# Token rows of six steps in flight, weight requests in another order, and 26 unread turns on TensorE, in a two-block gated decoder kernel

## The chip, the cores and the metric

The kernel runs on one core of a Trainium2 chip. The metric is the device time of one execution in microseconds (us). Five engines work side by side, each through its own list of instructions: PE (TensorE, matrix products; PEld is its loading of weights), DVE (VectorE), ACT (ScalarE), POOL (GpSimd) and SP (SyncE, which here only issues DMAs). They wait for each other through semaphores. "Granted clock" is the share of 2.4 GHz that TensorE is given; it has two levels, 1.00 and 0.50.

## The reference

Four sequences of 256 tokens with 256 channels pass through four gated parts, each added to x. The changed lines belong to the first two.

```python
# 1: state-space scan over 16 states on the context, gated by silu of the normalised x
x = x + tanh(g_xattn[0]) * scan_block(ctx, layernorm(x), ...)
# 2: mixture of experts: E=64 experts, K=8 per token, at most CAP=64 tokens per expert
logits = layernorm(x) @ gate_w.T
w, sel = top_k(softmax(logits), 8);  w = w / sum(w)
pos  = position of each (token, choice) in its expert's queue     # cumulative sum of one-hots
inp  = rows of x placed at (expert, pos) where pos < 64
h    = silu(inp @ wg[e]) * (inp @ wu[e])                           # 256 -> 96
out  = h @ wd[e]                                                   # 96 -> 256
y[token] += out[expert, pos] * w
# 3: attention of 16 heads over the context
# 4: two ternary linear layers with gelu and layer norm
```

## The kernel before

Everything is in one program with a hand-written instruction list for each engine. The parts that matter here:

*The scan* (up to about 162 us) works on two halves of 512 columns; 64 steps of DVE's scan instruction bound it. TensorE sums the products with turns of the identity (`add_pair`).

*The choice of experts, second half of tokens* (about 162 to 200 us). Behind the scan TensorE turns the gated output (`turn_out(1, b)`), waits while DVE adds it to x and takes the statistics, turns the normalised rows (`turn_normal(1, k)`), waits while ACT copies them out of PSUM, and makes the logits (`logits_of(1)`). Among these stand turns and products for the attention part, which fold its weight matrices (`turn_kv`, `fold_out`, `turn_wq`). DVE picks the experts, TensorE counts positions (`cumulate`, `count`, `lay_out`), and the result is `idx_x`, for each slot of each expert the index of its token row.

*The sixteen expert steps* (about 200 to 280 us). A step is a group of four experts, 256 slots. For step g:
- POOL's `take_rows(g)` gathers 2 x 128 rows of 320 numbers (256 of the token, 64 shares of the experts) from the table `token_rows` in HBM. They go to `xe`, a ring of RING = 4 places in the tile G. From step 4 on it waits for `hg_ready`, the gated product of step g - 4, which has used its rows.
- TensorE turns the rows (`turn_rows`), ACT copies them, TensorE multiplies with both weights (`gate_up`), ACT takes the silu, DVE the product, TensorE turns it (`turn_h`), multiplies with the down weights (`down`, two steps later), and adds the outputs into the token rows of the first sequence (`combine`, three steps later).
- SP's `put` writes the output of a step to the table `expert_out` in HBM, through three result tiles in turn.

In TensorE's list, turn g of the loop holds `turn_rows(g + 1)`, `gate_up(g)`, `turn_h(g - 1)`, `down(g - 2)` and `combine(g - 3)`.

*Weights.* Each group has 2 x 384 KB of gate and up weights and 384 KB of down weights. Groups 0 to 3 fill the ring at the start; 5 to 7 go to `wgu_early` and `wdn_early`, 15 to `wgu_last` and `wdn_last`, all before the stage or at its start. Group 4's gate and up weights go to `wgu_more`, the rest of the tile G behind `xe`, once the attention weights below it have been turned (`wqT_in_psum`). Groups 8 to 14 are requested in SP's loop over s, where each waits for `gu_done` or `down_done` of the group whose place it takes. A DMA issued by SP stands in one queue behind those issued before it.

Of the kernel before, what the change touches and what calls it, by code (L numbers as in the profile page):

```python
# [15 lines left out]
P = 128  # L16
# [24 lines left out]
B, L, H, DM = 4, 256, 256, 128  # L41
# [10 lines left out]
GROUP = 4  # L52
RING = 4
NG = E // GROUP
EARLY = 3
# [5 lines left out]
def build_program(nc, t, out):  # L61

    with ExitStack() as ctx:
# [168 lines left out]
        def gate_up_weights(slot):  # L232

            return (wgu[:, slot] if slot < RING else
                    (wgu_last[:], wgu_more, *(w[:] for w in early_gate_up))[slot - RING])

        def gate_up_slot(g):

            if g == NG - 1:
                return RING  # L240
            if RING <= g <= RING + EARLY:
                return g + 1
            return g % RING

        def down_weights(slot):
            return wdn[:, slot] if slot < RING else (wdn_last[:], None, *(w[:] for w in early_down))[slot - RING]

        def down_slot(g):

            if g == NG - 1:  # L250
                return RING
            if RING < g <= RING + EARLY:
                return g + 1
            return g if g < RING else 0 if g == RING else (g - RING - EARLY) % RING
# [5 lines left out]
        xe_flat = G[:].rearrange("p a k h -> p (a k h)")[:, 0:RING * 2 * ROW]  # L260
        wgu_more = G[:].rearrange("p a k h -> p (a k h)")[:, RING * 2 * ROW:].rearrange("p (a e i) -> p a e i", a=2, e=GROUP)
# [57 lines left out]
        def gate_up_landed(g):  # L319

            if g < RING:
                return d_w[g], 48
            if g == NG - 1:
                return d_ffn, 48
            if g == RING:
                return d_zero, 64
            if g <= RING + EARLY:
                return early_landed[g - RING - 1]
            return d_w[g % RING], 48 + 32 * (g // RING - 1)

        def down_landed(g):

            if g < RING:
                return d_w[g], 48
            if g == NG - 1:
                return d_ffn, 48
            if RING < g <= RING + EARLY:
                return early_landed[g - RING - 1]
            s, before = down_ring[down_slot(g)]
            return s, before + 16 * (1 if g < 12 and g != 11 else 2)  # L340
# [35 lines left out]
        d_gath = [[sem(f"d_gath{cc}{half}") for half in range(2)] for cc in range(2)]  # L376
        eo_hi_ready, eo_lo_ready = sem("eo_hi_ready"), sem("eo_lo_ready")
# [48 lines left out]
        def _(sp_):  # L426
# [21 lines left out]
            def gate_up_load(g):  # L448

                slot = gate_up_slot(g)  # L450
                if g == RING:
# [3 lines left out]
                landed = gate_up_landed(g)[0]  # L455
                for k, name in enumerate(("L0_ffn_wg", "L0_ffn_wu")):
                    dma(gate_up_weights(slot)[:, k],
                        t[name][g * GROUP:g * GROUP + GROUP].rearrange("e (p j) i -> p e (j i)", j=2))\
                        .then_inc(landed, 16)

            def down_load(g):

                if g == RING:
                    sp_.wait_ge(down_done, 1)
                elif RING + EARLY < g < NG - 1:
                    sp_.wait_ge(down_done, g - 6 if g < 12 else g - 3)
                dma(down_weights(down_slot(g))[0:I], t["L0_ffn_wd"][g * GROUP:g * GROUP + GROUP]
# [16 lines left out]
            gate_up_load(NG - 1)  # L484
            down_load(NG - 1)
# [32 lines left out]
            gate_up_load(RING)  # L518
# [2264 lines left out]
```

## Time and profile before

| | |
|---|---|
| median of 3 runs | 581.57 us (579.41 to 582.18) |
| the profiled execution | 579.86 us |
| its span, first to last instruction | 577.9 us |
| mean granted clock | 0.953 |
| busy: PE, DVE, ACT, POOL | 83%, 82%, 63%, 49% of the span |
| DMA | 48.63 MB, 84 GB/s over the span |
| the chain that ended last | PE 37%, DVE 21%, issue 20%, POOL 9%, ACT 7%, DMA 3% |

The profile is of one execution. The chain goes back from the last instruction to what released it, or to the one before it on its engine. "Issue" is time in which an engine waited for nothing that the profile shows. In a timeline a row's bracket is the engine's idle time before it and what ended it. PE records begin when a product begins; their ends overlap the next. A window has, for each engine, busy time and the number of instructions, then the granted clock, the DMA engines' share and the rate in GB/s. One `matmul` with 32-bit numbers over several columns can be two records.

### The profile page before, as it was taken

How to read it: one execution, taken by the hardware profiler on the slowest of the kernel's cores; microseconds unless marked ns; L12 is line 12 of the kernel's file. 1: busy time of each engine (PE TensorE's matmuls, PEld its weight loads, DVE VectorE, ACT ScalarE, POOL GpSimd, SP SyncE). 2: the span in 40 equal slices, each digit the busy share in tenths (PEclk: the TensorE clock that was granted, in tenths of full speed). 3: DMA queues.
4: the chain of work that ended last, by engine and by line, in shares of the span. 5: the costliest groups of instructions: out<-in, count | busy, mean ns of one | idle time of the engine just before them, and what ended most of it. 6: DMA issues, size and time to landing. Idle time of an engine off the chain costs nothing.

```text
span 577.9 us, 10286 instructions
## 1 busy us (share of the span) xinstructions
PE 478.6 (83%) x3070; PEld 361.1 (62%) x3080; DVE 473.6 (82%) x1249; ACT 365.2 (63%) x831; POOL 280.9 (49%) x263
## 2 busy tenths in 40 slices
PE   5817777757769889999899999998789988998735
PEld 3302222122348856776788999997689878997714
DVE  4899999999995737888666856996899969875887
ACT  2785555535434645688776666679656796679543
POOL 4118777869420465550278368623875243323211
PEclk9956999999997989999999999999999999999877
DMA  5939400001052979894412012400335000000000
GB/s 155 233 76 325 120 0 1 1 1 36 1 157 80 308 217 294 212 313 144 180 52 73 2 29 65 56 1 2 47 55 66 0 2 2 19 2 0 1 19 20
DMA packets 45626, 48.63 MB, mean 84 GB/s; under 512 B 5660, under 2 KB 42118, under 8 KB 45574
## 3 DMA queue, kind: packets, MB, share of 16 engines
q1 hardware_dynamic: 41734, 36.46, 22.2%
q0 software_dynamic: 3840, 11.54, 9.3%
q8 instruction: 25, 0.41, 0.3%
q14 instruction: 27, 0.22, 0.1%
HBM read 41.43 MB, written 6.56 MB: 83 GB/s over the span
## 4 chain that ended last, share of the span: by engine, by line
PE 37%; DVE 21%; issue 20%; POOL 9%; ACT 7%; DMA 3%; SPq 1%; DVEq 1%; POOLq 0%; ACTq 0%; another core or an unknown queue 0%
DVE hst L1880 7%; PE ps L1619 6%; PE ps L1558 5%; PE ps L1559 5%; PE ps L1560 5%; PE ps L1608 3%; PE ps L1476 2%; DMA G<-token_rows,idx_x 2%; POOL dbu L586 2%; PE ps L1277 2%; POOL G L672 2%; POOL pn L688 2%; DVE hc L1889 2%; POOL G L650 1%; PE ps L1374 1%
## 5 line engine op out<-in xcount | busy, mean ns | idle before, releaser
L688 POOL TENSOR_TENSOR pn<-pr,pinv 128x512 f32<-128x512 f32 x64 | 67.7, 1060 | 87.3 <-DVE pinv L2289 86.9
L586 POOL TENSOR_TENSOR dbu<-du,brow 128x512 f32<-128x512 f32 x64 | 81.5, 1285 | 41.4 <-DVE du L1873 23.1
L1277 PE MATMUL ps<-hc,ident 128*128 128x512 f32 x128 | 72.7, 657 | 27.5 <-DVE hc L1889 26.0
L1880 DVE TENSOR_TENSOR_SCAN hst<-ps,dbu 128x512 f32<-128x512 f32 x64 | 77.6, 1213 | 0.2 <-POOL dbu L586 0.2
L831 ACT ACTIVATE ps<-dtv,amat 128x510 f32<-128x510 f32 x64 | 44.1, 690 | 49.1 <-DVE hst L1880 48.2
L1019 ACT ACTIVATE pr<-ebuf,smin 128x256 f32<-128x256 f32 x128 | 63.7, 501 | 13.7 <-DVE smin L2280 6.9
L1619 PE MATMUL ps<-pT,cS 128*128 128x256 f32 x256 | 66.5, 382 | 0.0
L1277 PEld LDWEIGHTS ps<-hc,ident 128*128 128x128 f32 x128 | 20.3, 195 | 66.8 <-DVE hc L1889 63.6
L650 POOL DMA_INDIRECT G<-token_rows,idx_x x32 | 38.1, 1192 | 48.3 <-DVE wkv L2015 24.0
L672 POOL DMA_INDIRECT G<-expert_out,idx_g x48 | 51.6, 1074 | 11.6 <-issue 10.2
L2280 DVE CUSTOM_DVE_ANT_0 ebuf<-ps,mbias 128x256 f32<-128x256 f32 x128 | 48.9, 419 | 4.1 <-issue 4.0
L1558 PE MATMUL ps<-xnT,mqk 128*128 128x256 f32 x128 | 46.3, 362 | 6.7 <-DVE qT L2250 3.5
L1608 PE MATMUL ps<-ident,pn 128*128 128x128 f32 x256 | 39.4, 277 | 9.1 <-POOL pn L688 5.2
L1619 PEld LDWEIGHTS ps<-pT,cS 128*128 128x128 f32 x256 | 44.3, 191 | 3.7
L1033 ACT ACTIVATE oT<-ps 128x256 fp32r<-128x256 f32 x64 | 24.4, 382 | 31.8 <-PE ps L1619 31.7
L1558 PE MATMUL ps<-cT,qT 128*128 128x256 f32 x128 | 41.5, 324 | 1.4 <-DVE smin L2280 1.2
L1889 DVE TENSOR_TENSOR hc<-hst,ps 128x512 f32<-128x512 f32 x64 | 42.1, 659 | 0.0
L1027 ACT ACTIVATE pT<-ps 128x512 f32<-128x512 f32 x64 | 37.3, 583 | 4.3 <-PE ps L1608 4.2
L1558 PE MATMUL ps<-nvo,oT 128*128 128x256 f32 x128 | 37.2, 291 | 2.5 <-DVE oT L2250 2.5
L2250 DVE TENSOR_TENSOR oT<-ps,oT 128x256 fp32r<-128x256 f32 x64 | 26.7, 418 | 15.1 <-ACT oT L1033 14.8
L1608 PEld LDWEIGHTS ps<-ident,pn 128*128 128x128 f32 x256 | 29.1, 142 | 12.6 <-POOL pn L688 6.5
L1012 ACT ACTIVATE qT<-ps 128x256 fp32r<-128x256 f32 x64 | 24.6, 384 | 19.1 <-PE ps L1560 19.1
(380 smaller groups left out, 1377.3 us busy)
## 6 DMA issues: line engine op xcount, KB each, us to landing
wdn<-in_L_ffn_wd SPq DMA_DIRECT2D x12, 384.0 KB, 9.6
wgu<-in_L_ffn_wg SPq DMA_DIRECT2D x11, 384.0 KB, 7.0
wgu<-in_L_ffn_wu SPq DMA_DIRECT2D x11, 384.0 KB, 9.7
expert_out<-xn SPq DMA_DIRECT2D x11, 256.0 KB, 6.8
wq<-in_L_xattn_Wq SPq DMA_DIRECT2D x2, 1024.0 KB, 9.2
wo<-in_L_xattn_Wo SPq DMA_DIRECT2D x1, 2048.0 KB, 15.7
wo<-in_L_ffn_w SPq DMA_DIRECT2D x2, 1024.0 KB, 7.0
expert_out<-pexp SPq DMA_DIRECT2D x5, 256.0 KB, 3.3
```

The lines of the kernel that those rows point to most:

```text
L586: nc.gpsimd.tensor_tensor(dbu[:, j, :], du[:, j % 2, 512 * hb:512 * hb + 512], brow[:, j // 2, :], ALU.mult).then_inc(pool_dbu, 1)
L672: nc.gpsimd.indirect_dma_start(G[:, cc, k, :], None, eout, bass.IndirectOffsetOnAxis(ap=idx_g[:, col:col + 1], axis=0), bounds_check=SLOTS ...
L688: nc.gpsimd.tensor_tensor(pn[:, h % 2], pr[:, h % 2], pinv[:, h % 2, :].unsqueeze(2).to_broadcast([P, 2, L]), ALU.mult)\
L831: A(bank(d).rearrange("p (b l) -> p b l", b=2)[:, :, 1:], dtv[:, d, 512 * hb:512 * hb + 512].rearrange("p (b l) -> p b l", b=2)[:, :, 1:], ...
L1019: last = A(pr[:, h % 2, tt, :], sneg[:, h % 2, tt, :], ACT.Exp, scale=-1.0, bias=smin[:, h % 2, tt:tt + 1], accum_out=psum_[:, h % 2, tt:t ...
L1277: pe.matmul(bank(2 + j % 2), ident[:], hc[:, j % 2, :], start=(isinstance(m, int) and m + k == 0), stop=(isinstance(m, int) and m + k == N ...
L1558: pe.matmul(o, lhs[0], rhs[0], start=start, stop=False)
L1608: last = pe.transpose(ps[:, 4, L * st + P * tt:L * st + P * tt + P], pn[:, h % 2, tt, P * st:P * st + P], ident[:])
L1619: last = pe.matmul(ps[:, 3 + 2 * (h % 2), 0:L], cS[:, b % 2, st, :], pT[:, h % 2, st, :], start=(st == 0), stop=(st == 1))
L1880: V.tensor_tensor_scan(hst[:, j, :], bank(j % 2), dbu[:, j, :], 0.0, ALU.mult, ALU.add)\
L1889: V.tensor_tensor(hc[:, j % 2, :], hst[:, j, :], bank(6 + j // 2), ALU.mult).then_inc(hc_ready, 1)
L2280: last = V.tensor_tensor_reduce(sneg[:, h % 2, tt, :], ps[:, 1, L * tt:L * tt + L], mbias[:, b, :], -(DH ** -0.5), 3e38, ALU.add, ALU.min, ...
```

## The change

Four things:
1. `xe` gets ROWS = 6 places instead of four. `take_rows(g)` waits for the gate of step g - 6; steps 4 and 5 wait for `wqT_in_psum`, since their places were group 4's weights. The two new places use the semaphores of the later gathers, `d_gath[0]`, whose counts in `add_choices` start 64 higher.
2. Homes of weights: group 4 takes what was group 15's (`wgu_last`, `wdn_last`), and groups 8 to 15 follow in a ring of five. `wgu_more` is gone.
3. SP requests group g's gate and up weights in turn (6g - 36) // 5 + 1 of its loop, the down weights one turn later.
4. On TensorE, `gate_up(1)` and `gate_up(2)` stand ahead of `turn_rows(2)` and `turn_rows(3)`; and `keep_busy` turns the identity into a PSUM tile that nobody reads, 12, 9 and 5 times, at three places of the choice of experts. It was there before, with 24 such turns written out, behind the expert steps.

```diff
+ROWS = 6
-        xe = G[:].rearrange("p a k h -> p (a k h)")[:, 0:RING * 2 * ROW].rearrange("p (s q w) -> p s q w", s=RING, q=2)
-        wgu_more = G[:].rearrange("p a k h -> p (a k h)")[:, RING * 2 * ROW:].rearrange("p (a e i) -> p a e i", a=2, e=GROUP)
+        xe_flat = G[:].rearrange("p a k h -> p (a k h)")[:, 0:ROWS * 2 * ROW]
+        xe = xe_flat.rearrange("p (s q w) -> p s q w", s=ROWS, q=2)
+        def home(g):
+            if g < 2 * RING:
+                return g
+            return (g - 2 * RING) % (RING + 1)
...
             def gate_up_load(g):
-                if g == RING:
-                    sp_.wait_ge(wqT_in_psum, NKV)
-                elif RING + EARLY < g < NG - 1:
-                    sp_.wait_ge(gu_done, g - 7 if g < 12 else g - 3)
+                if g > RING + EARLY:
+                    sp_.wait_ge(gu_done, g - 7 if g <= 3 * RING else g - 4)
...
-            gate_up_load(NG - 1)
-            down_load(NG - 1)
+            gate_up_load(RING)
+            down_load(RING)
...
             down_load(RING + 1)
-            gate_up_load(RING)
             for s in range(NG + 2):
-                if s < 2:
-                    gate_up_load(s + 8)
-                if s == 2:
-                    down_load(RING)
-                    gate_up_load(10)
...
+                for g in range(2 * RING, NG):
+                    if s == (6 * g - 36) // 5 + 1:
+                        gate_up_load(g)
+                    if s == (6 * g - 36) // 5 + 2:
+                        down_load(g)
                 if s > 1:
                     put(s - 2)
...
             def take_rows(g):
-                if g >= RING:
-                    pool.wait_ge(hg_ready, g - RING + 1)
+                if g >= ROWS:
+                    pool.wait_ge(hg_ready, g - ROWS + 1)
+                elif g >= RING:
+                    pool.wait_ge(wqT_in_psum, NKV)
...
+            def keep_busy(k, count):
+                for _ in range(count):
+                    pe.transpose(ps[:, k, 0:P], ident[:], ident[:])
...
             turn_kv(1)
+            pe.wait_ge(b_copied, 2 * NS)
+            keep_busy(4, 12)
             turn_out(1, 0)
...
             fold_out(1)
+            keep_busy(6, 9)
             turn_normal(1, 0)
             turn_normal(1, 1)
+            keep_busy(4, 5)
             logits_of(1)
...
             for g in range(NG + 3):
+                if g in (1, 2):
+                    gate_up(g)
                 if g + 1 < NG:
                     turn_rows(g + 1)
-                if 0 < g < NG:
+                if 2 < g < NG:
                     gate_up(g)
```

TensorE behind the scan, before: `ps<-ident,wkv` is `turn_kv`, `ps<-ident,u` is `turn_out`, `ps<-wo,w2T` is `fold_out`, `ps<-ident,xn` is `turn_normal`, `ps<-gwT,dtv` is `logits_of`.

```order
L1366 MATMUL ps<-ident,wkv 128x128 x8
L1289 MATMUL ps<-ident,u 128x128 x8
...
L1374 MATMUL ps<-wo,w2T 128x256 x4
L1301 MATMUL ps<-ident,xn 128x128 x8
L1310 MATMUL ps<-gwT,dtv 128x64 x8
L1374 MATMUL ps<-wo,w2T 128x256 x4
```

The same place in the changed kernel, where `ps<-ident` is a filler:

```order
L1346 MATMUL ps<-ident,wkv 128x128 x8
L1258 MATMUL ps<-ident 128x128 x12
L1269 MATMUL ps<-ident,u 128x128 x8
...
L1354 MATMUL ps<-wo,w2T 128x256 x4
L1258 MATMUL ps<-ident 128x128 x9
L1281 MATMUL ps<-ident,xn 128x128 x8
L1258 MATMUL ps<-ident 128x128 x5
L1290 MATMUL ps<-gwT,dtv 128x64 x8
L1354 MATMUL ps<-wo,w2T 128x256 x4
```

Nothing else has moved there; 26 rows were added.

TensorE at the start of the expert steps, before (`ps<-ident,G` turns rows, `ps<-wgu,ebuf` is gate and up, `ps<-ident,ebuf` is `turn_h`, `ps<-wdn,hT` is down):

```order
L1464 MATMUL ps<-ident,G 128x128 x4
L1476 MATMUL ps<-wgu,ebuf 64x192 x8
L1464 MATMUL ps<-ident,G 128x128 x4
L1541 MATMUL ps<-wabs,ones 128x2
L1464 MATMUL ps<-ident,G 128x128 x4
L1476 MATMUL ps<-wgu,ebuf 64x192 x8
L1487 MATMUL ps<-ident,ebuf 96x128 x2
L1464 MATMUL ps<-ident,G 128x128 x4
L1476 MATMUL ps<-wgu,ebuf 64x192 x8
L1487 MATMUL ps<-ident,ebuf 96x128 x2
L1497 MATMUL ps<-wdn,hT 64x256 x4
```

And in the changed kernel:

```order
L1448 MATMUL ps<-ident,G 128x128 x4
L1459 MATMUL ps<-wgu,ebuf 64x192 x8
L1448 MATMUL ps<-ident,G 128x128 x4
L1525 MATMUL ps<-wabs,ones 128x2
L1459 MATMUL ps<-wgu,ebuf 64x192 x8
L1448 MATMUL ps<-ident,G 128x128 x4
L1470 MATMUL ps<-ident,ebuf 96x128 x2
L1459 MATMUL ps<-wgu,ebuf 64x192 x8
L1448 MATMUL ps<-ident,G 128x128 x4
L1470 MATMUL ps<-ident,ebuf 96x128 x2
L1479 MATMUL ps<-wdn,hT 64x256 x4
```

Gate and up of steps 1 and 2 now stand ahead of the turning of the rows of the step after.

SP's list behind the request of group 5, before (`expert_out<-` rows are puts):

```order
L457 DMA G<-in_L_ffn_wg 128x4x192
L457 DMA G<-in_L_ffn_wu 128x4x192
L457 DMA wgu<-in_L_ffn_wg 128x4x192
L457 DMA wgu<-in_L_ffn_wu 128x4x192
L457 DMA wgu<-in_L_ffn_wg 128x4x192
L457 DMA wgu<-in_L_ffn_wu 128x4x192
L467 DMA wdn<-in_L_ffn_wd 96x4x256
L457 DMA wgu<-in_L_ffn_wg 128x4x192
L457 DMA wgu<-in_L_ffn_wu 128x4x192
L511 DMA expert_out<-xn 128x2x256
```

And in the changed kernel:

```order
L493 DMA expert_out<-xn 128x2x256
L441 DMA wgu<-in_L_ffn_wg 128x4x192
L441 DMA wgu<-in_L_ffn_wu 128x4x192
L493 DMA expert_out<-xn 128x2x256
L449 DMA wdn<-in_L_ffn_wd 96x4x256
L441 DMA wgu<-in_L_ffn_wg 128x4x192
L441 DMA wgu<-in_L_ffn_wu 128x4x192
L493 DMA expert_out<-pexp 128x2x256
```

Nine requests (3.5 MB) that stood ahead of the first put are behind it or, those of group 4, far ahead of the stage.

## Rows read from the trace of the kernel before

**Rows 1.** Timeline of TensorE, 146 to 206 us: start us, us, engine, line, operation [idle before].

```profile
151.97 1.89 PE L1310 MATMUL ps<-gwT,dtv 128*128 128x64 f32 x16
...
164.86 1.09 PE L1289 MATMUL ps<-ident,u 128*128 128x128 f32 x8 [1.86 <-DVE u L2045]
...
167.53 1.97 PE L1374 MATMUL ps<-wo,w2T 128*128 128x256 f32 x8
170.86 1.38 PE L1301 MATMUL ps<-ident,xn 128*128 128x128 f32 x8 [1.36 <-DVE xn L2054]
172.93 3.67 PE L1310 MATMUL ps<-gwT,dtv 128*128 128x64 f32 x16 [0.69 <-ACT dtv L850]
176.39 3.50 PE L1374 MATMUL ps<-wo,w2T 128*128 128x256 f32 x8
...
183.06 0.19 PE L1330 MATMUL ps<-ebuf,through 128*128 128x64 bf16 x1
```

**Rows 2.** Windows: PE, PEld, DVE, ACT, POOL busy, granted clock, DMA share, GB/s.

```profile
164.00:166.00 2.00, 1.14 (x10) 1.15 (x11) 1.93 (x6) 0.00 (x0) 0.26 (x1) 1.00 0.04 6
172.00:174.00 2.00, 1.31 (x7) 1.08 (x7) 1.93 (x12) 1.32 (x3) 0.00 (x0) 0.68 1.13 288
206.00:208.00 2.00, 1.44 (x8) 1.03 (x10) 0.00 (x0) 0.38 (x1) 1.39 (x3) 0.71 1.12 370
```

**Rows 3.** Timeline of TensorE from 200 us, columns as in rows 1.

```profile
200.42 0.74 PE L1464 MATMUL ps<-ident,G 128*128 128x128 f32 x4 [0.69 <-ACT mqk_full L861]
201.94 1.52 PE L1476 MATMUL ps<-wgu,ebuf 128*64 128x192 f32 x16 [0.78 <-ACT ebuf L919]
203.39 0.75 PE L1464 MATMUL ps<-ident,G 128*128 128x128 f32 x4
...
206.56 1.03 PE L1464 MATMUL ps<-ident,G 128*128 128x128 f32 x4 [2.30 <-DMA G<-token_rows,idx_x]
207.51 2.83 PE L1476 MATMUL ps<-wgu,ebuf 128*64 128x192 f32 x16
...
224.25 0.75 PE L1464 MATMUL ps<-ident,G 128*128 128x128 f32 x4 [1.17 <-DMA G<-token_rows,idx_x]
...
228.81 0.64 PE L1464 MATMUL ps<-ident,G 128*128 128x128 f32 x4
...
232.20 0.39 PE L1512 MATMUL ps<-eo_hi,place 128*128 128x256 f32 x1
...
233.25 0.65 PE L1464 MATMUL ps<-ident,G 128*128 128x128 f32 x4
...
280.35 2.79 PE L1554 MATMUL ps<-ident 128*128 128x128 f32 x24
```

**Rows 4.** Chain of waits, 140 to 290 us: start us, us, what.

```profile
215.79 8.42 DMA G<-token_rows,idx_x
```

**Rows 5.** Timelines of ACT and of DVE, 155 to 212 us, columns as in rows 1.

```profile
178.45 0.60 ACT L861 ACTIVATE nvo_full<-ps 128x512 f32<-128x512 f32 x1 [5.09 <-PE ps L1374]
...
180.93 0.30 DVE L1948 TENSOR_SCALAR ebuf<-left 128x256 bf16<-128x256 f32 x1
```

**Rows 6.** Timeline of POOL, 190 to 262 us, one gather of 128 rows each.

```profile
194.93 1.28 POOL L650 DMA_INDIRECT G<-token_rows,idx_x  x1 [23.96 <-DVE wkv L2015]
...
205.21 1.00 POOL L650 DMA_INDIRECT G<-token_rows,idx_x  x1 [0.30 <-issue]
...
211.88 1.00 POOL L650 DMA_INDIRECT G<-token_rows,idx_x  x1 [3.05 <-DVE ebuf L2136]
```

**Rows 7.** Line L650, the row gathers that began at 206 to 208 us.

```profile
DMA to landing us min/median/max: 3.0/3.6/4.5
```

**Rows 8.** Windows in the expert steps, columns as in rows 2.

```profile
214.00:216.00 2.00, 2.00 (x20) 1.54 (x20) 1.19 (x5) 1.93 (x4) 1.39 (x3) 1.00 0.89 194
...
250.00:260.00 10.00, 10.00 (x87) 7.55 (x86) 9.32 (x18) 8.37 (x19) 4.72 (x4) 1.00 1.10 298
```

**Rows 9.** DMA issues at 223 to 224 us: engine, operation, count, size, us to landing.

```profile
expert_out<-pexp SPq DMA_DIRECT2D x1, 256.0 KB, 10.9
```

More of the change, by code:

```diff
@@ L230, in build_program, with gate_up_weights, down_weights @@
         prep_scope.close()
[L232 to L254, printed above, removed]
+        gate_up_homes = [*(wgu[:, k] for k in range(RING)), wgu_last[:], *(w[:] for w in early_gate_up)]
+        down_homes = [*(wdn[:, k] for k in range(RING)), wdn_last[:], *(w[:] for w in early_down)]
+        def home(g):
+            if g < 2 * RING:
+                return g
+            return (g - 2 * RING) % (RING + 1)
+        def gate_up_weights(g):
+            return gate_up_homes[home(g)]
+        def down_weights(g):
+            return down_homes[home(g)]
         G = sb("G", [P, 2, K, H])
-        xe = G[:].rearrange("p a k h -> p (a k h)")[:, 0:RING * 2 * ROW].rearrange("p (s q w) -> p s q w", s=RING, q=2)
-        xe_flat = G[:].rearrange("p a k h -> p (a k h)")[:, 0:RING * 2 * ROW]
-        wgu_more = G[:].rearrange("p a k h -> p (a k h)")[:, RING * 2 * ROW:].rearrange("p (a e i) -> p a e i", a=2, e=GROUP)
+        xe_flat = G[:].rearrange("p a k h -> p (a k h)")[:, 0:ROWS * 2 * ROW]
+        xe = xe_flat.rearrange("p (s q w) -> p s q w", s=ROWS, q=2)
         spare = sb("spare", [P, 2])
@@ L322, in gate_up_landed @@
                 return d_w[g], 48
-            if g == NG - 1:
+            if g == RING:
                 return d_ffn, 48
-            if g == RING:
-                return d_zero, 64
             if g <= RING + EARLY:
                 return early_landed[g - RING - 1]
-            return d_w[g % RING], 48 + 32 * (g // RING - 1)
+            if home(g) == RING:
+                return d_ffn, 48 + 32 + 32
+            return d_w[home(g)], 48 + 32 * (1 if g < 3 * RING else 2)
         def down_landed(g):
[L333 to L340, printed above, removed]
+            if g <= RING + EARLY:
+                return gate_up_landed(g)
+            if home(g) == RING:
+                return d_zero, 32 + 16
+            s, before = down_ring[home(g)]
+            return s, before + 16 * (1 if g < 3 * RING else 2)
         d_rows = sem("d_rows")
@@ L658, in _ @@
             pool.wait_ge(idx_x_ready, 1)
-            for g in range(RING):
-                take_rows(g)
-            for g in range(RING, NG):
+            for g in range(NG):
                 take_rows(g)
@@ L1498, in down @@
                                          hT[:, g % 2, P * q + CAP * e:P * q + CAP * e + CAP],
-                                         down_weights(slot)[0:I, 2 * q + e, :], start=True, stop=True)
+                                         down_weights(g)[0:I, 2 * q + e, :], start=True, stop=True)
                 last.then_inc(down_done, 1)
@@ L1708, in tail_turn_hidden @@
                 last.then_inc(f_hqT_in_psum, 1)
-            def keep_busy(k, count):
-                for _ in range(count):
-                    pe.transpose(ps[:, k, 0:P], ident[:], ident[:])
             def tail_out(k, first=0, end=FT):
@@ L2210, in add_choices @@
                     if k < 2:
-                        dve.wait_ge(d_gath[cc][half], 8 * K * b)
+                        dve.wait_ge(d_gath[cc][half], 8 * K * b + (0 if cc else 64))
                 if k > 1:
```

38 lines of the change are left out of this document (13 added, 25 removed).

## The prediction

> **What bounds the kernel now.** I read the page's forty slices for stretches in which no engine is full, then the chain of waits from 140 to 290 us, then TensorE's timeline in the two stretches that the change touches, and last the windows for the granted clock and the DMA rate. The two stretches are the choice of experts of the second half of the tokens (162 to 200 us) and the sixteen expert steps (200 to 284 us). Before and behind them nothing is changed, so everything behind them should only move with them.
>
> In the first stretch TensorE is busy without a gap from 172.93 on, but it starts that run slowly. It idles 1.86 us before the turns at 164.86, 1.36 before those at 170.86 and 0.69 before the logits at 172.93 [rows 1]. The granted clock is 1.00 (2.4 GHz) at 164 to 166, and falls to the half level (1.2 GHz) within 172 to 174 (mean 0.68) [rows 2]. The same logits that take 1.89 us at 151.97 take 3.67 at 172.93, and four folding products that take 1.97 at 167.53 take 3.50 at 176.39 [rows 1].
>
> In the second stretch a step of TensorE is 4.45 us (228.81 to 233.25), of which the combining products are the last 1.05 (232.20 to 233.25); a step without them is 3.40. From 224.25 on the steps follow with hardly a gap. Before that they don't: 2.30 us are lost before 206.56 and 1.17 before 224.25, both to token rows that had not landed, and gate-and-up of step 1 takes 2.83 us instead of 1.52 [rows 3], because the first of these waits let the clock fall to a mean of 0.71 in 206 to 208 [rows 2]. The piece of the chain that ends in the second wait is a landing of 8.42 us [rows 4]. That is the landing of step 6's rows. So this stage is TensorE's, apart from a ragged start.
>
> **The fillers.** They add 12, 9 and 5 turns that nobody reads. The 24 turns of the same kind at 280.35 take 2.79 us [rows 3], 0.116 each, so the three fillers are 1.40, 1.05 and 0.58 us and stand in gaps of 1.86, 1.36 and 0.69. Each begins when its gap begins: the wait on b_copied that the first brings forward has long been met (its last copy belongs to the scan, which has ended), and the instruction behind each filler waits for something from DVE or ACT that the filler doesn't touch. What hides them is these waits, with 0.46, 0.31 and 0.11 us to spare. Without that cover they would cost up to 3.03 us, at the half clock twice that. I take 0.
>
> What they may give is the clock. If it doesn't fall, the logits get back 3.67 - 1.89 = 1.78 us and the four products 3.50 - 1.97 = 1.53, together 3.31. Does another engine stand in the way? ACT's copy at 178.45, which waited 5.09 us for TensorE's products, sits ahead of the exponentials; it follows TensorE. DVE's choice at 180.93 begins 2.48 us behind that copy and takes 0.30 [rows 5]. With the faster clock TensorE ends the first pair of products near 172.93 + 1.78 + 0.95 = 175.7; the choice is then ready at 175.7 + 2.48 + 0.30 = 178.5. TensorE wants it for the counting products, which began at 183.06 [rows 1], now 3.31 earlier at 179.75. So 1.25 us are to spare and TensorE stays the bound up to the row indices. The row gathers on POOL begin at 194.93 behind these [rows 6] and come 3.3 us earlier too; so do the stage's weight requests, all of them behind waits on TensorE. Bounds: 0 if the clock falls all the same, 3.31 if it holds, and -1.5 if a filler runs late. I take 3.3, since all three gaps shrink to less than half a microsecond, and TensorE held full clock at 164 to 166, right behind its longest gap [rows 1, 2].
>
> The engine's turns in the gaps are themselves transposes, as are those at 164.86, and the clock read 1.00 around them. The Trainium skill (TensorE: Matmul & The Clock Gate, "Part 4: PE-mode transpose") says against this that the full clock does not engage for the transpose mode. By that rule the fillers give nothing, and the sum would end 3.3 us later; by the rows it holds. It is part of the first rival below.
>
> **Six steps of rows in flight, and two gate-and-ups moved ahead.** From here I count in the time of the old trace, leaving the 3.3 out. Turns to gate-and-up is 201.94 - 200.42 = 1.52 us (ACT copies between them), gate-and-up is 203.39 - 201.94 = 1.45 [rows 3]. In the old order gate-and-up of step 1 stands behind the turns of step 2 and so behind their late rows. In the new one it stands ahead: start 203.39 + 1.52 = 204.91, end 206.36. The rows of step 2 had landed at 206.51 and should land a little earlier, since two requests for weights that stood in front (those of group 4 and of group 8) are gone from there. Turns of step 2 at 206.4, gate-and-up of step 2 at 207.9 to 209.35, then the rest of a step without combining, 3.40 - 1.45 = 1.95, gives 211.3. Step 3 and step 4 at 4.45 (or 3.40 + 1.05) give 215.75 and 220.2 for the start of step 5, the one that began at 224.25. That is 4.05 us. It holds the 2.30 and 1.17 of waiting and the slow clock of 207 to 210 less the 0.7 and 0.6 us of new idling while ACT copies; these are too short to bring the clock down again, to judge by 164 to 166.
>
> Do the rows keep up? POOL issues a gather in 1.00 us and 0.30 between two; the eighth, at 205.21, stands 10.28 us behind the first, so 1.47 each at the worst [rows 6]. A step is 2.6 to 2.9 us, less than a step of TensorE. In the old order step 5's rows waited 3.05 us at 211.88 for step 1's gate [rows 6]; now the first such wait is step 6's, for step 0's gate, which is past. The gathers at 206 to 208, the last of step 4 among them, landed in 3.0 to 4.5 us [rows 7]: step 4's rows are there at 210.8 to 212.3 and wanted at 211.3. Step 6's second gather is the fourteenth: 205.21 + 6 x 1.3 = 213.0, not 215.79, and wanted landed at 220.2. It has 7.2 us, against 8.42 in the old trace behind a bunch of weight requests [rows 4] and 3.0 to 4.5 without one. Bounds of this part: 4.05 less 1.0 (step 4 late) and 1.2 (step 6 late) is 1.85; 4.05 plus the 0.6 of idling if ACT's copy hides better is 4.65. I take 4.05, as the requests that slowed those landings come later now.
>
> **Later weight requests.** The same eight groups (8 to 15, and 4 traded for 15) are fetched in the stage, 3 x 384 KB each, but the first request moves from step 0 to behind the first put, which follows the down of step 0 (211.3) and ACT's copies of it, about 212.7. From there to gate-and-up of step 15, at 220.2 + 10 x 4.45 = 264.7, there have to land: gate and up of eight groups (6.3 MB), down of seven (2.75), nine puts of 256 KB (2.4) and eleven steps of rows (256 rows of 1,280 bytes, 3.6): 15.0 MB in 52 us, 289 GB/s. Measured under full load: 298 at 250 to 260, but 194 at 214 to 216 [rows 8]. At 298 all is there 1.7 us before it is needed; at 280, 1.6 late; at 194 it would be 25 late. The stage of before was loaded to the brim for a shorter time only, with a put that landed in 10.9 us [rows 9], and no step was late for a weight. I take 0.5 us lost, from the 298 of the longer of these windows and some unevenness. Behind a late weight all of TensorE's queue would wait, and with it ACT's takings-out.
>
> **The sum.** 579.86 (span 577.9 and 2.0 around it) - 3.3 - 4.05 + 0.5 = 573.0. The profiled execution is 1.7 us below the median 581.57 of the three runs. The clock is one reason why runs differ: in it the fillers' 3.3 was paid in full, in others perhaps not. I add half the distance and say 573.9.
>
> **The rivals.**
> 1. *The clock falls anyway* at the logits, or the fillers' turns don't count for it. Against it speaks that the gaps shrink to a fourth or less; for it, that I see only one fall in this place. Then 573.9 + 3.3 = 577.2.
> 2. *The DMA queues take the place of the rows.* Mechanism: requests are bunched into steps 3 to 12, the load is above what is delivered, and from about step 13 TensorE waits for gate-and-up weights, or ACT for the landing of a put three steps back. It decides below 289 GB/s. At 270 GB/s 15.0 MB take 55.6 us, 3.6 late in place of the 0.5 counted: 577.0. To end slower than before by 2.9 us it needs over 11 us of lateness, 15.0 MB in 63 us, 238 GB/s; at 229 it ends at 587. Before had a stretch as bad (194), but only for 2 us.
> 3. *The ragged start was not on the path:* the gathers are paced by POOL at 2.6 us a step, so TensorE only waits elsewhere. Then of the 4.05 only the slow clock's 1.3 is won: 576.6. Against it: 2.6 is well below 3.40.
> 4. *It doesn't do what it says:* no change, 581. The fillers late by as much as the start wins would do it; I see no row for it.
>
> **How the numbers follow.** Both gains: 0.60, its own range 571.5 to 576. Rival 1: 0.12. Rival 2 at a few microseconds: 0.10, with a true slowdown 0.05. Rival 3: 0.08. Rival 4: 0.05. Half a per cent of 581.57 is 2.9 us, about what a measurement here tells from nothing: faster is below 578.7, slower above 584.5. The forecast, rivals 1 and 3 and most of the mild rival 2 are below 578.7: 0.86. Within: 0.09. Slower: 0.05. The range that leaves out two in ten: 570.5 to 578.5.
>
> **What would show it.** Granted clock 1.00 from 160 to 200 us and logits of about 1.9 us; the row gathers from about 191.6. No wait of TensorE over 1 us between the first turns of rows and the last combining; gate-and-up of step 1 at 1.5 us; step 5 starting near 216.9; and everything behind the stage about 7 us earlier. DMA share near 1 from 210 to 250 us, with puts landing in 10 to 12 us. Wrong it would be if the logits are still near 3.6 us, or if TensorE waits for weights in steps 12 to 15.

## The result: slower where it was first timed, faster on four chips timed later

The changed kernel took 583.36 us (median of 20 runs, 580.97 to 586.37) where the kernel before took 579.53 (20 runs, 576.52 to 582.89): ratio 1.0065, 95% interval 1.0046 to 1.0085. That is 0.65% slower, clear of the noise. On which chip this was is not recorded. I had forecast 573.9, range 570.5 to 578.5. The forecast is wrong, in its sign too. The profiled execution took 583.94 us with a span of 582.0, against 579.86 and 577.9 before.

TensorE's timeline of the changed kernel, in the stretches of [rows 1] and [rows 3] (columns as there):

```profile
172.91 2.00 PE L1290 MATMUL ps<-gwT,dtv 128*128 128x64 f32 x16
174.75 1.95 PE L1354 MATMUL ps<-wo,w2T 128*128 128x256 f32 x8
...
198.91 0.74 PE L1448 MATMUL ps<-ident,G 128*128 128x128 f32 x4 [2.38 <-issue]
200.43 2.83 PE L1459 MATMUL ps<-wgu,ebuf 128*64 128x192 f32 x16 [0.78 <-ACT ebuf L894]
...
208.44 1.52 PE L1459 MATMUL ps<-wgu,ebuf 128*64 128x192 f32 x16 [1.30 <-issue]
209.89 0.75 PE L1448 MATMUL ps<-ident,G 128*128 128x128 f32 x4
...
215.63 1.63 PE L1459 MATMUL ps<-wgu,ebuf 128*64 128x192 f32 x16 [3.08 <-issue]
...
283.00 2.79 PE L1538 MATMUL ps<-ident 128*128 128x128 f32 x24
```

The reader is to see two halves. Up to 196.5 us all went as forecast: the logits take 2.00 us instead of 3.67 and four folding products 1.95 instead of 3.50 [rows 1]. The gathers then begin 3.2 us earlier (191.73, against 194.93 in [rows 6]). From there on the gain is lost. The first turns of rows come only 1.51 us earlier than in [rows 3]. TensorE then stands still three times (2.38, 1.30 and 3.08 us) without a releaser that the trace can name ("issue"). The 24 turns behind the stage come at 283.00, 2.65 us later than before instead of 6.9 earlier.

The gathers on POOL in the same stretch, the first and the last three of the sixteen:

```profile
191.73 1.28 POOL L627 DMA_INDIRECT G<-token_rows,idx_x  x1 [20.78 <-DVE wkv L1994]
...
209.82 1.00 POOL L627 DMA_INDIRECT G<-token_rows,idx_x  x1 [0.31 <-issue]
211.13 1.00 POOL L627 DMA_INDIRECT G<-token_rows,idx_x  x1 [0.30 <-issue]
212.44 1.00 POOL L627 DMA_INDIRECT G<-token_rows,idx_x  x1 [0.30 <-issue]
```

ACT and then DVE there:

```profile
198.26 0.60 ACT L836 ACTIVATE mqk_full<-ps 128x512 f32<-128x512 f32 x1 [2.16 <-remote]
...
207.74 0.60 ACT L894 ACTIVATE ebuf<-ps 128x512 f32<-128x512 f32 x1 [3.17 <-PE ps L1448]
...
214.93 0.60 ACT L894 ACTIVATE ebuf<-ps 128x512 f32<-128x512 f32 x1 [6.11 <-remote]
```

```profile
215.78 0.35 DVE L2115 TENSOR_TENSOR ebuf<-ebuf,ps 128x192 f32<-128x192 f32 x1 [6.57 <-ACT ebuf L899]
```

TensorE turned the rows of step 3 at 209.89 and was done at 210.64; ACT, which had been idle, copied them at 214.93. The profile also records when a semaphore changed. The change that tells ACT "turned" is recorded at 214.91: it came 4.27 us behind the end of TensorE's work, and ACT began 0.02 us behind the change. So ACT did not dawdle, the signal was late (TensorE's ends are modelled, but 18 of the 20 profiles show no such distance over 0.1 us). The copies at 198.26 and 207.74 begin late in the same way, behind signals that came 1.70 and 0.81 us late. POOL issued gathers as if nothing were wrong. The windows show what the stalls did to the clock (columns as in [rows 2]):

```profile
200.00:204.00 4.00, 3.57 (x22) 2.68 (x22) 1.25 (x4) 0.65 (x3) 3.09 (x4) 0.59 0.38 104
...
212.00:216.00 4.00, 0.92 (x9) 0.76 (x10) 0.21 (x1) 1.07 (x4) 1.13 (x2) 1.00 0.31 95
216.00:220.00 4.00, 4.00 (x26) 2.11 (x22) 3.70 (x12) 2.53 (x8) 2.48 (x3) 0.61 0.43 117
220.00:224.00 4.00, 4.00 (x24) 3.37 (x25) 2.06 (x6) 1.88 (x4) 1.70 (x2) 0.53 0.99 283
```

Behind two of the stalls TensorE runs at the half level (1.2 GHz). The DMA share, 0.31 to 0.46 in the windows of 4 us from 200 to 220, says that the queues were not full. From 227 on the steps follow at 4.45 us, as forecast.

### The profile page after: what moved, and what is told of

It is laid out like the page before. It is cut to its first block, busy times and chain, and to the rows that moved or that the text cites. A ratio compares the mean times of both kernels' runs of the same rounds, so it can differ in the third digit from the quotient of the medians.

```text
span 582.0 us, 10348 instructions
## 1 busy us (share of the span) xinstructions
PE 485.9 (83%) x3106; PEld 366.4 (63%) x3106; DVE 473.5 (81%) x1249; ACT 363.3 (62%) x831; POOL 279.1 (48%) x263
## 4 chain that ended last, share of the span: by engine, by line
PE 35%; DVE 24%; issue 24%; POOL 8%; ACT 7%; DMA 1%; SPq 1%; DVEq 1%; POOLq 0%; ACTq 0%
DVE hst L1859 8%; PE ps L1603 5%; PE ps L1542 4%; PE ps L1543 4%; PE ps L1544 4%; PE ps L1459 3%; PE ps L1592 3%; POOL dbu L561 2%; DVE hc L1868 2%; POOL G L647 2%; POOL pn L663 2%; PE ps L1479 1%; PE ps L1494 1%; PE ps L1448 1%; DMA x<-in_x 1%
## 5 line engine op out<-in xcount | busy, mean ns | idle before, releaser
L627 POOL DMA_INDIRECT G<-token_rows,idx_x x32 | 36.8, 1149 | 43.7 <-DVE wkv L1994 20.8
L1542 PE MATMUL ps<-xnT,mqk 128*128 128x256 f32 x128 | 47.1, 368 | 6.5 <-DVE qT L2229 3.3
L1543 PE MATMUL ps<-xnT,mqk 128*128 128x256 f32 x128 | 36.6, 286 | 0.0
```

The lines of the kernel that those rows point to most:

```text
L1542: pe.matmul(o, lhs[0], rhs[0], start=start, stop=False)
L1543: pe.matmul(o, lhs[0], rhs[1], start=False, stop=False)
```

## The experiments

Each run has the median of its kernel, with lowest and highest time in brackets, and its ratio to the kernel before on the same chip, with the 95% interval. Its profile is of one execution. A "stall" is an idle stretch of TensorE over 1 us for which the trace names no releaser.

Theory A, after this profile: sixteen gathers issued without a pause, with no other request on the queues, hold back the signals of the other engines. Theory B: the earlier start meets a quiet queue of SP. Theory C: the rows are late.

### Four partial versions, on chip 5 (before: 578.21 us, 35 runs)

**e1, the fillers alone.** The kernel before, with the three calls added:

```
+            pe.wait_ge(b_copied, 2 * NS)
+            keep_busy(4, 12)    # ahead of the turns at [rows 1] 164.86
...
+            keep_busy(6, 9)     # ahead of those at 170.86
...
+            keep_busy(4, 5)     # ahead of the logits
```

> The kernel before with nothing but the three fillers (12, 9 and 5 turns of the identity). The fillers keep the granted clock at 1.00 through the logits and the folding products, so the row gathers begin 3.2 us earlier; if that is a gain by itself: 576.2, that is 3.3 us below before. Theory B: the gain is given back in the expert stage, because what is late there comes at a fixed time or stalls: within 1 us of before.

575.47 us (574.42 to 577.02), ratio 0.9956 (0.9930 to 0.9981): by the ratio 2.5 us of my 3.3. The gathers come 2.14 us earlier. The logits began 1.04 us later in this execution (173.97), and from there to the first gather it is 18.82 us, where it was 22.00. The late rows of before are there, but by 1.29 us and not 2.30:

```profile
203.79 0.75 PE L1473 MATMUL ps<-ident,G 128*128 128x128 f32 x4 [1.29 <-DMA G<-token_rows,idx_x]
```

**e2, all but the fillers** (the three calls taken out of the changed kernel).

> The changed kernel without its three fillers. Theory A, the stalls of TensorE in the expert stage (results handed on 1.7 and 4.9 us late in the changed kernel's profile) come from the rows and requests alone: the stalls are there again, the clock falls at the logits, and it takes 3 us longer than the changed kernel, 586 to 587. Theory B, the earlier start of the gathers brings the stalls: no stall over 1 us, and 576 to 580.

578.22 us (573.28 to 581.89), ratio 1.0004 (0.9967 to 1.0042). Sixteen gathers and more run without a pause from 197.05 on, and no stall is in the trace.

**e3, rows paced as before.**

```
                 if g >= ROWS:
-                    pool.wait_ge(hg_ready, g - ROWS + 1)
+                    pool.wait_ge(hg_ready, g - RING + 1)
                 elif g >= RING:
                     pool.wait_ge(wqT_in_psum, NKV)
+                    pool.wait_ge(hg_ready, g - RING + 1)
```

> The changed kernel, but each gather of rows waits for the gate four steps back, as before, so POOL pauses between gathers; homes, requests and order stay changed. Theory A, the unbroken run of 16 gathers holds TensorE's results back: the stalls go and the time is 574 to 577. Theory B, the quiet queue of SP (no weight request for 30 us) or its later bunch does it: 583, like the changed kernel. Theory C, rows are late again without six in flight: 577 to 580 with waits on rows as before.

574.39 us (573.16 to 578.44), ratio 0.9943 (0.9914 to 0.9973), no stall. The profiled execution (577.88) is one of the slowest of its runs; in it the rows of step 4 are 1.32 us late.

**e4, TensorE's order of before.**

```
-                if g in (1, 2):
-                    gate_up(g)
                 if g + 1 < NG:
                     turn_rows(g + 1)
-                if 2 < g < NG:
+                if 0 < g < NG:
                     gate_up(g)
```

> The changed kernel with gate-and-up of steps 1 and 2 back behind the turns of the next rows. If the order brings nothing and the stalls are elsewhere: 583 to 584. If the order itself is what goes wrong: below 580. If the order gives the 1.5 us it was priced at: 585.

576.00 us (573.13 to 578.15), ratio 0.9958 (0.9926 to 0.9991). POOL's sixteen gathers run unbroken (and at least six more behind them), and again nothing stalls; TensorE waits once for rows, as it did before:

```profile
203.21 0.74 PE L1448 MATMUL ps<-ident,G 128*128 128x128 f32 x4 [1.31 <-DMA G<-token_rows,idx_x]
```

Each part taken away made the kernel "faster than changed" by 5 to 9 us. Three different parts can't each be the cause by itself; at most all of them together could be. What I had not done was to time the changed kernel itself beside them.

### The changed kernel once more, and three more versions, on chip 14 (before: 578.66 us)

**e5, the changed kernel, unaltered.**

> The changed kernel once more, not a character altered, now on the chip and in the hour of its partial versions (which took 574.4 to 578.2 us beside a before of 578.2). Theory A (the three parts together bring the stage's first steps under an unbroken run of sixteen gathers with no other request on the queues, and TensorE's, ScalarE's and VectorE's results are then held back for 2 to 6 us): ratio to before 1.0065 again, within 0.003, and in the profile idle stretches of TensorE without a releaser between 198 and 218 us that sum to over 5 us. Theory D (the stalls belonged to the job in which it was first timed, not to the kernel): ratio 0.990 to 0.997 like its partial versions, no idle stretch without a releaser over 1.2 us there.

574.50 us (572.62 to 576.92), ratio 0.9924 (0.9895 to 0.9953). Theory A falls, since the three parts together bring no stall here. Theory D (the stalls belong to the first timing) holds: the forecast of 573.9 is missed by 0.6. The expectation says "on the chip of its partial versions"; it ran on chip 14, and e1 to e4 on chip 5. The timeline of TensorE:

```profile
197.98 0.75 PE L1448 MATMUL ps<-ident,G 128*128 128x128 f32 x4 [0.69 <-ACT mqk_full L836]
199.50 1.52 PE L1459 MATMUL ps<-wgu,ebuf 128*64 128x192 f32 x16 [0.78 <-ACT ebuf L894]
...
205.42 1.52 PE L1459 MATMUL ps<-wgu,ebuf 128*64 128x192 f32 x16 [0.52 <-issue]
206.87 0.75 PE L1448 MATMUL ps<-ident,G 128*128 128x128 f32 x4
...
209.46 1.52 PE L1459 MATMUL ps<-wgu,ebuf 128*64 128x192 f32 x16
...
213.91 1.52 PE L1459 MATMUL ps<-wgu_last,ebuf 128*64 128x192 f32 x16
...
273.80 2.79 PE L1538 MATMUL ps<-ident 128*128 128x128 f32 x24
```

and ACT's copy of step 3's turns:

```profile
207.65 0.60 ACT L894 ACTIVATE ebuf<-ps 128x512 f32<-128x512 f32 x1 [1.85 <-PE ps L1448]
```

Here "turned" takes 0.03 us (turns done at 207.62, copy at 207.65), where it took 4.29. From the first turns of rows to the 24 turns it is 75.82 us; before it was 79.93 [rows 3], in the first profile of the changed kernel 84.09.

**e6, weight requests two steps earlier.**

```
-                    if s == (6 * g - 36) // 5 + 1:
+                    if s == (6 * g - 36) // 5 - 1:
                         gate_up_load(g)
-                    if s == (6 * g - 36) // 5 + 2:
+                    if s == (6 * g - 36) // 5:
                         down_load(g)
```

> The changed kernel, with each later weight request two steps earlier in SyncE's program (gate 8's gate-up matrices at step 1 instead of 3, its down matrices at step 2 instead of 4, and so on), so that weights move while the sixteen gathers are issued, as they did before the change. Theory A (quiet queues and unbroken gathers hold results back): the stalls of 198 to 218 us shrink, and the time is 3 to 8 us below that of the changed kernel in this batch. Theory D (the stalls are no property of the kernel): equal to the changed kernel within 1.5 us. Theory Q (transfers that share the queues with the gathers slow the rows): slower by 1 to 3 us, with turn_rows waiting for DMA.

577.34 us (575.65 to 582.49), ratio 0.9989 (0.9960 to 1.0017), 2.8 above e5. Theory Q had the size but not the reason. It isn't the rows: ACT waits for puts of three steps back, which crowd with the weights:

```profile
240.12 0.84 ACT L914 ACTIVATE xn<-ps,wkv 128x256 f32<-128x256 f32 x2 [1.63 <-DMA expert_out<-xn]
246.06 0.84 ACT L914 ACTIVATE pexp<-ps,wkv 128x256 f32<-128x256 f32 x2 [2.43 <-DMA expert_out<-pexp]
251.51 0.84 ACT L914 ACTIVATE xn<-ps,wkv 128x256 f32<-128x256 f32 x2 [1.94 <-DMA expert_out<-xn]
257.59 0.84 ACT L914 ACTIVATE xn<-ps,wkv 128x256 f32<-128x256 f32 x2 [2.57 <-DMA expert_out<-xn]
```

That is my rival 2 in small. In e5 the longest such wait of ACT is 0.86 us, at 261.56.

**e7, fillers and later requests** (the edits of e3 and e4 together).

> The changed kernel without six steps of rows in flight (the gathers of step g wait for the gates of step g-4, as before) and with gate-up 1 and 2 back behind the transposes: what is left is the fillers and the later weight requests. The fillers alone gave 575.5, ratio 0.9956. If the later requests cost what I predicted (0.5 us) the ratio is 0.9965; if they are free or gain, 0.993 to 0.9955. No stalls by theory A, since the gathers of steps 4 to 7 are spread out: turn_rows of steps 4 to 7 waits for rows 1 to 3 us in all instead.

575.89 us, ratio 0.9945 (0.9921 to 0.9970), beside 0.9956 for the fillers alone: in the medians the later requests cost nothing that can be told. But in the profiled execution, the slowest of its runs (577.73), TensorE does wait for weights:

```profile
260.60 1.52 PE L1460 MATMUL ps<-wgu,ebuf 128*64 128x192 f32 x16 [1.44 <-DMA wgu<-in_L_ffn_wu]
```

That is what rival 2 described. Such waits (0.7 to 1.4 us) are in three profiles, all with rows paced as before (e3, e7, e12), and in none with six steps of rows in flight.

**e8, six steps of rows and later requests** (the edits of e2 and e4 together).

> The changed kernel without fillers and with gate-up 1 and 2 back behind the transposes: six steps of rows and later requests are left. My prediction's sum gives this pair -3.5 us at most (six rows) +0.5, so a ratio of 0.995; theory A gives 1.000 as for the kernel without fillers (0.9967 to 1.0042), since the unbroken run of gathers is there, but the stage starts 3.2 us later; theory E (only gate-up 1 and 2 ahead of the transposes bring stalls) gives 0.993 to 0.997 and none in the profile.

576.71 us (572.92 to 581.33), ratio 0.9967 (0.9932 to 1.0003).

### Is it the company or the chip?

**e9, the changed kernel, with only the kernel before beside it.**

> The changed kernel again, unaltered, now the only kernel beside the one before, as when it was first timed (583.4 us, ratio 1.0065, with 7 us of stalls in its profile), and loaded afresh. In the batch of four it took 574.5 us, ratio 0.9924. Theory D (the first time belongs to that load of the program or to that chip): ratio 0.990 to 0.996 here, no idle stretch of TensorE without a releaser over 1.2 us between 198 and 218 us. Theory F (the stalls come when this program and the one before are alone on the chip, since the programs then lie at the same places in memory as the first time): ratio 1.003 to 1.010 and the stalls at 198, 208 and 215 us again. Theory A (a property of the kernel) has fallen with the batch of four unless the stalls come back here.

582.95 us (580.22 to 586.35, 10 runs) beside 578.72, ratio 1.0070 (1.0039 to 1.0101), on chip 1. The slowdown is back, and so are the stalls, to within 0.01 us of the first profile. The three late signals are there as well (1.72, 0.81 and 4.28 us, beside 1.70, 0.81 and 4.27):

```profile
199.59 0.74 PE L1448 MATMUL ps<-ident,G 128*128 128x128 f32 x4 [2.39 <-issue]
...
209.17 1.52 PE L1459 MATMUL ps<-wgu,ebuf 128*64 128x192 f32 x16 [1.31 <-issue]
...
216.36 1.52 PE L1459 MATMUL ps<-wgu,ebuf 128*64 128x192 f32 x16 [3.08 <-issue]
...
280.69 2.79 PE L1538 MATMUL ps<-ident 128*128 128x128 f32 x24
```

So it is nothing random. Theory F (what lies on the chip beside the program) and theory G (the chip) both allowed it.

**e10, the same once more.**

> The changed kernel unaltered, once more with no other changed kernel beside it. So far: 583.4 and 583.0 us alone (stalls of 2.4, 1.3 and 3.1 us in front of turn_rows(0), gate_up(2) and gate_up(3), equal in both profiles to 0.01 us), 574.5 us in a batch of four on another chip (no such stalls). Theory F (what else is loaded decides where program and data lie, and that decides the stalls): 581 to 586 us and the same three stalls, whatever the chip. Theory G (the chip decides): either result, the same whenever the chip is the same.

575.81 us (572.63 to 578.32), ratio 0.9945 (0.9905 to 0.9986), on chip 0, first turns to the 24 turns in 75.81 us and no stall. Theory F falls: the company was the same as in e9. What differed is the chip (and that the program was loaded anew).

### Eight runs on chips without stalls

These runs were to find out on a chip with stalls which part of the change they need. None of them came onto such a chip, so that stays open; they give each part's share on undisturbed chips.

**e11 to e14, on chip 12 (before: 579.12 us):** the changed kernel, then the edits of e3, e4 and e2.

> The changed kernel unaltered, beside its partial versions on one chip. By theory G (the chip decides; so far stalled on chip 1 and in the first job, not on chips 0 and 14) either 583 us with stalls of 2.4, 1.3 and 3.1 us before turn_rows(0), gate_up(2) and gate_up(3), or 574 to 576 us without. It is the yardstick for the other three.

> The changed kernel with the gathers of steps 4 and on waiting for the gates of four steps before, as before the change. If the chip stalls the changed kernel: theory A+G (on such a chip the unbroken run of sixteen gathers is what is punished) gives 574 to 577 us here; if any early start of the gathers stalls there, 580 to 583. If the chip does not stall it: 574.4 as on chip 5, within 1 us of the changed kernel.

> The changed kernel with gate-up 1 and 2 back behind the transposes. On a chip that stalls the changed kernel: 580 to 584 us if the unbroken gathers are what is punished, 575 to 577 if the order on TensorE is. On another chip 576, as on chip 5, 1 to 2 us above the changed kernel, which is what the moved gate-ups save.

> The changed kernel without the fillers. On a chip that stalls the changed kernel: 586 us if the stalls come whenever sixteen gathers run unbroken, 578 if they come only with the start that is 3.2 us earlier. On another chip 578.2, as on chip 5, 3.5 us above the changed kernel: the fillers' share of the gain.

e11 575.58 us, ratio 0.9927 (0.9898 to 0.9956). e12 575.34, 0.9930 (0.9898 to 0.9961). e13 576.25, 0.9964 (0.9932 to 0.9996). e14 577.57 (572.69 to 580.39), 0.9964 (0.9924 to 1.0004). The profile of e14 holds a surprise. There are no fillers, the gaps are as long as in [rows 1], and the clock did not fall:

```profile
165.25 1.06 PE L1269 MATMUL ps<-ident,u 128*128 128x128 f32 x8 [1.91 <-issue]
...
171.21 1.38 PE L1281 MATMUL ps<-ident,xn 128*128 128x128 f32 x8 [1.36 <-DVE xn L2030]
173.28 2.00 PE L1290 MATMUL ps<-gwT,dtv 128*128 128x64 f32 x16 [0.69 <-ACT dtv L825]
```

In e8, with the same gaps, it fell:

```profile
172.00:176.00 4.00, 3.31 (x17) 2.99 (x17) 3.57 (x20) 1.68 (x3) 0.00 (x0) 0.65 1.08 311
176.00:180.00 4.00, 4.00 (x14) 3.37 (x14) 0.98 (x3) 0.90 (x2) 0.00 (x0) 0.50 0.11 39
```

**e15 and e16, on chip 9 (before: 578.63 us):** the changed kernel and the edit of e3.

> The changed kernel unaltered, on whatever chip this is: 583 us with the three stalls on a chip like chip 1, 574 to 576 us without them on one like chips 0, 12 and 14. Yardstick for the run beside it.

> The changed kernel with the gathers of steps 4 and on paced by the gates of four steps before. On a chip that stalls the changed kernel: 574 to 578 us and no idle stretch of TensorE without a releaser over 1 us if sixteen unbroken gathers are what the stalls need; 580 to 583 us and the stall before turn_rows(0) in any case if they need only the early start. On another chip 574 to 575.5.

574.71 us, ratio 0.9952 (0.9912 to 0.9991), and 577.11, 0.9979 (0.9948 to 1.0009).

**e17 and e18, on chip 12 again (before: 578.58 us):** the same pair.

> The changed kernel unaltered on one more chip: 583 us with the three stalls, as in the first job and on chip 1, or 574 to 576 us without, as on chips 0, 9, 12 and 14. Yardstick for the run beside it.

> The changed kernel with the gathers of steps 4 and on paced by the gates of four steps before. Where e17 stalls: 574 to 578 us if the stalls need sixteen gathers without a pause, 580 to 583 us if they need only the early start. Elsewhere: 574 to 577 us, 0 to 2.5 us above e17 as on chips 12 and 9.

575.15 us, ratio 0.9945 (0.9913 to 0.9977), and 576.21, 0.9965 (0.9928 to 1.0002). In the profiled execution of e17, 577.33 us and the slowest of its runs, a row of step 4 is late and the clock falls behind it. That is the bound "step 4 late" of my range, priced at 1.0 us; the stage took 3.3 us longer than in e5 (79.08, against 75.82):

```profile
210.57 0.85 PE L1448 MATMUL ps<-ident,G 128*128 128x128 f32 x4 [1.63 <-DMA G<-token_rows,idx_x]
211.35 2.83 PE L1459 MATMUL ps<-wgu,ebuf 128*64 128x192 f32 x16
```

No version beat the changed kernel beside it beyond what can be told: e12 lay 0.2 us below e11, e16 and e18 lay 2.4 and 1.1 above.

## Why the prediction was wrong, and where it was right

**The fillers (-3.3).** Right in mechanism in the first profile too: clock 1.00 and 3.2 us won up to the gathers. From the start of the logits to the first gather it is 18.81 or 18.82 us in every profile with fillers and in e14, and 22.00 to 22.13 in before, e2 and e8. None of the sixteen profiles with fillers shows the fall at 172 to 180 us; of four without (before, e2, e8, e14) three do. The price was right, but it was taken as paid in every execution. On average it is less: 2.5 us in e1, 2.0 between e14 and e11. The lists of times say the same: e2 and e14 spread over 573 to 582 us and e1 over 574.4 to 577.0. The fillers take away a fall that comes in some executions. Rival 1 would have left the logits near 3.67. (One slip in the working: the end of the first products was worked out with the 1.78 us saved instead of the 1.89 that the logits take. It changes 0.1 of 1.25 us to spare.) The rule of the Trainium skill (TensorE: Matmul & The Clock Gate, "Part 4: PE-mode transpose"), by which the full clock does not engage for transposes, did not decide here: 26 turns of the identity stand in the gaps, the granted clock stayed at 1.00 and the logits behind them took 2.00 us. Whether these turns, which the rows call MATMUL, ran in the mode that the page means can't be told from them. And since e14 held the clock without them, one profile alone proves nothing; it is the sixteen against three falls in four that speak for the fillers.

**Six rows and the order (-4.05), in the run that decided.** This is the step that failed. I took it for granted, without a term or a reason, that a signal of TensorE arrives when its work ends. I forecast that the first turns come at 200.42 - 3.3 = 197.1 and the following steps without waits of over 1 us. Against e5, the same program without stalls, the first profile lost:
- 1.69 us before the first turns: folding ended 0.76 us earlier (196.53, against 197.29), and the turns began 0.93 later. ACT's copy between them got its signal 1.70 us late.
- 5.24 us from there to gate-and-up of step 3 (16.72 us, against 11.48): 1.31 at the half clock in 200.43, 0.78 and some 3.15 in the two later stalls.
- 3.03 us in the rest of the stage (84.09 - 75.82 - 5.24), where the clock read 0.61 and 0.53 in 216 to 224.
- 2.1 us behind the stage (299.0, against 296.9), with one more fall of the clock at 288 to 292 (0.57), and with signals up to 1.1 us late at 347 to 444 us:

```profile
288.00:292.00 4.00, 3.66 (x18) 3.69 (x19) 1.45 (x5) 1.17 (x4) 1.80 (x2) 0.57 0.96 372
```

Less the 0.76 that makes 11.3, the whole distance of the two spans (582.0 and 570.7). The prediction had no term or rival for that. Its only case of a slowdown, rival 2, was another mechanism: no step waited for a weight, and 250 to 260 us moved 280 GB/s at a clock of 1.00 (298 in [rows 8]).

**The same term on the other chips.** From the first turns to the 24 turns the working gives 79.93 - 4.05 + 0.5 = 76.4 us, and 75.9 without the 0.5 for late weights; e5, e10 and e15 show 75.82, 75.81 and 75.80. So the 4.05 held to 0.1 us against the profile it was read from, and the 0.5 was not paid. In e11 and e17 it is 77.28 and 79.08, with step 4's rows late by 1.41 and 1.63 us. The parts: with the order of before the stage takes 76.27 and 76.32 us (e4, e13), so the moved gate-and-ups give 0.5; with rows paced as before 79.29, 79.37, 77.94 and 75.86 (e3, e12, e16, e18), 0 to 3.5 more, weight waits of e3 and e12 among it. In the medians of chips 12 and 9 that pacing costs -0.2 to 2.4. But the profile that the 4.05 was read from was a bad case. With the fillers alone (e1) the stage took 78.12 us: the wait for step 2's rows was 1.29 and not 2.30. Of the six profiles with such a wait there (before, e1, e4, e7, e8, e13) only those two show the fall of the clock behind it. Against e1 the other three parts win 2.3 us, not 3.55.

**Later requests (+0.5).** They cost nothing in the medians beside e1 (e7), and no weight is late in any profile of the changed kernel. Asking earlier with six rows in flight costs 2.8 us (e6). Rival 2 named the right danger, the puts, on the other side of the choice. With later requests ACT waits for a put too, by up to 1.56 us in the changed kernel (e10, at 261.55), but the stage is not longer for it (75.81 us). A put at 223 us took 11.0 us in e5 too (10.9 in [rows 9]), and nobody waited for it.

**The sum.** On four chips without stalls the changed kernel took 574.5 to 575.8 us, 0.6 to 1.9 above the forecast and inside its range, ratios 0.9924 to 0.9952. By the medians the gain is 3.2 to 4.2 us and not 6.85; part of the hit is luck, since the medians of before lay lower than the 581.57 I started from. The two terms were read from one execution that paid both falls of the clock (172 and 206 us) in full; the experiments price them at 2.0 to 2.5 us and, one profile against another, some 2.3 us. That other executions of before escape these falls is likely but not shown: only one was profiled, and its mean clock, 0.953, is above the mean of the others on these chips (0.948 to 0.950). An average execution of before thus has more falls than this one, if at other places.

**What is shown and what is not.** Shown: the time belongs to the chip or to how the program was loaded there, since one text took 575 us on chips 0, 9, 12 and 14 and 583 on chip 1, and the stalls are there when it is slow and not when it is fast. Shown: unbroken gathers, the order and the early start don't bring stalls by themselves (e4, e5, e10).

Shown by the records of semaphore changes: it is TensorE's signals that are late, and only beside gathers. In the first profile 24 changes made by TensorE come over 0.1 us behind the end of their instruction, in e9 23, up to 4.89 us; in the other eighteen profiles none does. No recorded change made by ACT, DVE or POOL is late in any profile. All 47 late ones fall into stretches in which POOL issues gathers (or up to 3 us behind), most of them at 196 to 223 us and then, beside the gathers of `expert_out`, at 344 to 444 us. In each of the two profiles 435 changes of TensorE are recorded outside such stretches, none of them late. The stalled traces also hold fewer such records, 4,819 and 4,717, against 5,411 to 5,420 in each of the others. Up to the first gather they are complete (1,442 and 1,440, beside 1,441 in e5); they thin out from there to some 200 us behind the stage, and the end of the trace is complete again.

Code that is loaded late would be a rival. The traces don't show it: from 140 to 320 us the transfers of the instruction queues took 0.3 to 1.7 us each in the two stalled profiles as in e5 and e10.

Not shown: which part of the change the stalls need on such a chip, and what holds TensorE's signals back beside gathers there and not elsewhere. Chip and loading can't be parted either, as chip 1 came up once. The kernel before ran at 578.7 us on chip 1 as elsewhere, though it gathers as well; no profile of it was taken there.

## What to carry to other kernels

Time the changed kernel again beside its partial versions, and on more than one chip, before explaining a loss: three "cures" in a row had only run on another chip. A term read from one profiled execution is the full price of an event that may come in part of the executions; look whether the clock's fall is in every run (a wide or two-humped list of times says it isn't) and weigh the term with that. When engines idle together and no releaser is named, compare the end of the producer with the start of the consumer: 0.03 us is a signal, 4.3 us is something else. Where the trace records the semaphore's change, it tells which side of the signal was late.

## What the runs showed of the hardware that I had not expected

- A signal from TensorE to ACT, 0.03 us on one chip, took 4.3 us on another in the same program, and the three stalls agreed to 0.01 us in two profiles (2.38 and 2.39, 1.30 and 1.31, 3.08 and 3.08). Only TensorE's signals were late, and only beside gathers (47 of 47).
- The fall of TensorE's clock at one place is not fixed by the gaps before it: after gaps of 1.91, 1.36 and 0.69 us it stayed at 1.00 in e14, and fell in e8 and before. With fillers it fell once at another place, 160 to 164 us in e12, ahead of the first filler:

```profile
160.00:164.00 4.00, 3.52 (x7) 1.60 (x8) 2.61 (x15) 0.00 (x0) 0.00 (x0) 0.63 0.00 0
```
